# Queries and keys stacked along the contraction, through HBM, with no streamed matmuls ahead of the row scores

## What is computed

```
x = ln(x + splat_attention(x))        # 16-wide; scores = q_w . k_w, where q_w, k_w = exp(-distance to 16 centres)
x = ln(x + cross_attention(x, ctx))   # 16-wide, 120 keys
x = ln(x + one_of_8_experts(x))
x = ln(x + causal_attention(x))       # 16-wide, with biases
x = ln(x + block(x, ctx))             # self attention (32-wide, masked after the softmax) and an MLP,
                                      # then cross attention (32-wide, 120 keys) and an MLP
x = ln(x + four_of_16_experts(x))
attention: softmax(scale * q k^T) v, for each head
```

## Time and profile before

| | |
|---|---|
| median of three runs | 3835.8 us (3827.08 to 3843.56) |
| profiled execution | span 3842.1 us from the first to the last instruction; no separate time of the execution is given beside it |
| TensorE matmul busy | 3304.1 us, 86% of the span, 38960 instructions |
| VectorE, ScalarE, GpSimd busy | 2753.4, 2095.4 and 976.8 us |
| mean granted TensorE clock | 0.909 of 2.4 GHz |
| moved by DMA | 31.49 MB |

### The profile page before, as it was taken

One profiled execution on the slowest core, in us unless ns is written; L12 is line 12 of the kernel. 1 busy time (PEld: TensorE's weight loads), 2 busy tenths in 40 slices (PEclk: granted clock), 3 DMA queues, 4 the chain that ended last, 5 costly groups with the idle time before them and its releaser, 6 DMA issues. The chain is left out here.

```text
span 3842.1 us, 94561 instructions
## 1 busy us (share of the span) xinstructions
PE 3304.1 (86%) x38960; PEld 2345.7 (61%) x38960; DVE 2753.4 (72%) x6299; ACT 2095.4 (55%) x4222; POOL 976.8 (25%) x1792
## 2 busy tenths in 40 slices
PE   2989888889888888888988888899988898988886
PEld 1666666666665656666656666576655665666664
DVE  6777776777766767777767677677776777777755
ACT  5645655555456564564465555545555555466552
POOL 1312341122223321231133122212342122124310
PEclk9899998999989999999989898899988998999987
DMA  5000000000000000000000000000000000000000
GB/s 168 3 3 2 2 3 5 10 8 3 2 2 4 5 3 7 7 3 2 7 2 2 5 4 8 6 4 2 2 2 3 10 10 4 2 2 2 2 4 6
DMA packets 30365, 31.49 MB, mean 8 GB/s; under 512 B 8673, under 2 KB 26482, under 8 KB 29938
## 3 DMA queue, kind: packets, MB, share of 16 engines
q1 hardware_dynamic: 29938, 25.44, 2.2%
HBM read 21.24 MB, written 4.19 MB: 7 GB/s over the span
## 5 line engine op out<-in xcount | busy, mean ns | idle before, releaser
L1142 ACT ACTIVATE p<-bank,p_log 128x512 f32<-128x512 f32 (+2 forms) x1280 | 747.6, 584 | 1238.8 <-PE bank L834 1188.6
L1716 POOL TENSOR_TENSOR prob<-p,prob 120x256 f16<-120x256 f32 (+2 forms) x512 | 453.3, 885 | 1734.7 <-ACT prob L1143 1733.5
L1143 ACT ACTIVATE prob<-bank,p_log 128x512 f16<-128x512 f32 (+2 forms) x1280 | 748.2, 585 | 0.0
L1418 DVE TENSOR_REDUCE negm<-bank 128x2 f16<-128x512 f32 (+1 forms) x1280 | 675.5, 569 | 26.7 <-PE bank L789 15.6
L1336 DVE TENSOR_TENSOR prob<-p,prob 128x512 f16<-128x512 f32 (+2 forms) x768 | 467.4, 616 | 179.4 <-ACT prob L1143 175.7
L811 PE MATMUL bank<-q,k 32*128 32x256 f16 (+2 forms) x6144 | 491.0, 286 | 70.8 <-ACT prob L1143 28.0
L701 PE MATMUL bank<-w_exp,ident_h 128*128 128x512 f16 x1280 | 425.2, 417 | 16.6 <-DVE xa L1330 12.2
L1725 POOL TENSOR_SCALAR_AFFINE_SELECT probm<-prob 128x128 f16<-128x128 f16 x1024 | 328.1, 359 | 314.9 <-DVE prob L1336 314.9
L811 PEld LDWEIGHTS bank<-q,k 32*128 32x128 f16 (+1 forms) x6144 | 305.1, 109 | 150.2 <-issue 42.0
L834 PE MATMUL bank<-ident_h,negm 128*128 128x256 f16 (+2 forms) x2560 | 379.8, 270 | 0.0
L1708 POOL TENSOR_TENSOR rstd<-veps,minus_half 128x2 f32<-128x2 f32 (+2 forms) x192 | 146.3, 762 | 809.8 <-DVE veps L1304 809.1
(11 more groups left out here) (300 smaller groups left out, 6223.5 us busy)
## 6 DMA issues: line engine op xcount, KB each, us to landing
x<-in_x SPq DMA_DIRECT2D x16, 256.0 KB, 2.6
out<-z SPq DMA_DIRECT2D x16, 256.0 KB, 2.1
x<-in_li SPq DMA_DIRECT2D x7, 256.0 KB, 4.5
xa<-in_li SPq DMA_DIRECT2D x7, 256.0 KB, 4.5
z<-in_li SPq DMA_DIRECT2D x6, 256.0 KB, 4.6
x<-in_wq SPq DMA_DIRECT2D x4, 256.0 KB, 4.4
cx<-in_ctx_t SPq DMA_DIRECT2D x16, 60.0 KB, 1.8
cx<-in_ctx SPq DMA_DIRECT2D x16, 60.0 KB, 1.8
```

What stands on the lines that cost most here:

```text
L1142: act(p32[0:n, g % PBUF32, 0:cols], ps[0:n, 0:cols], ACT.Exp, bias=p_log[0:n, :], scale=a.scale)
L1143: act(prob[0:n, 0, g % PBUF, 0:cols], ps[0:n, 0:cols], ACT.Exp, bias=p_log[0:n, :], scale=a.scale).then_inc(a_done, one(a_done))
L1418: v.tensor_reduce(negm[:, h * NT:(h + 1) * NT], ring_v[bank_of(e, v_full)][:, :].rearrange("p (t n) -> p t n", t=NT)[:, :, 0:ATTNS[k].keys ...
L1716: g.tensor_tensor(prob[0:n, 1, m % PBUF, 0:cols], p32[0:n, m % PBUF32, 0:cols], prob[0:n, 0, m % PBUF, 0:cols], ALU.subtract).then_inc(pp_ ...
```

## The change

- Query and key parts of a head are stacked along the contraction. A stack of a 32-wide head has three planes, 96 rows: queries high, low, high against keys high, high, low. One of a 16-wide head has four planes and 16 rows of zeros, 80 rows: queries high, low, high, low against keys high, high, low, low. One matmul over the stack gives what three gave (with low by low added in the 16-wide ones).
- Row scores use the same stacks, so they are no longer of the high parts only. The heads of a pair come one after the other, as whole-height matmuls; `heads_of`, `at` and `parity` go.
- [...] `made` (one buffer, no longer two sets) takes the pair of parts; SP's queue stores each plane of it into `heads16` or `heads32` (four or three transfers for q, the same for k). `fill` brings four heads (a quad) back into one of three slots of `q_ring` and `k_ring`, two transfers a quad, four quads a phase. 
- ScalarE (in the splat attention VectorE) waits before it writes q into `made` until the keys of the phase before are stored, and before k until q is stored. A fill waits until k is stored, and for a slot until the exact scores of the quad three earlier are issued. PE waits for `ring_full` at each fourth head.
- Keys are made once. Those of the first cross attention take the short way from the bank; the causal ones are copied high by ScalarE.
- Exact scores are computed before the wait for the maxima, not after it.
- `STREAM_ROWS` is 0 instead of 2.
- At the start GpSimd clears a tile and SP writes eight transfers of zeros from it into the stacks' last 16 rows.

```diff
-STREAM_NORM, STREAM_GATES, STREAM_HEADS, STREAM_ROWS = 0, 0, 0, 2
+QUAD, QUADS, SLOTS = 4, 4, 3
+Q_PLANES = (0, 1, 0, 1)
+K_PLANES = {3: (0, 0, 1), 4: (0, 0, 1, 1)}
+STREAM_NORM, STREAM_GATES, STREAM_HEADS, STREAM_ROWS = 0, 0, 0, 0
...
-        qT = [pair(f"q{s}", 4, TOK) for s in range(SETS)]
-        kT = [pair(f"k{s}", 4, TOK) for s in range(SETS)]
+        made = pair("made", 4, TOK)
+        q_ring, k_ring = (sb(f"{what}_ring", [96, SLOTS, QUAD, TOK], F16) for what in "qk")
+        heads16 = {what: nc.dram_tensor(f"{what}_heads16", (2, 8, 80, 2, TOK), F16).ap() for what in "qk"}
+        heads32 = {what: nc.dram_tensor(f"{what}_heads32", (2, 4, 96, 4, TOK), F16).ap() for what in "qk"}
...
+                    for g in pair:
+                        a = ATTNS[ORDER[g][0]]
+                        if g % QUAD == 0:
+                            e.wait_ge(ring_full[g // QUAD % SLOTS], slot_filled(g // QUAD))
+                        q, kk = operands(g)
+                        ps = slot("v", "max", g)
...
+                        for i in range(NT):
+                            n = P if a.causal and i == 0 else a.keys
+                            last = mm(ps[:, i * TOK:i * TOK + n], q[:, i * P:i * P + P], kk[:, 0:n],
+                                      start=i == 0, stop=i == NT - 1 and not a.causal)
...
+                        for j, (k0, n) in enumerate(a.key_tiles):
+                            i0 = j * P if a.causal else 0
+                            mm(ps[0:n, j * TOK:j * TOK + TOK - i0], kk[:, k0:k0 + n], q[:, i0:TOK],
+                               start=j == 0, stop=False)
+                        e.wait_ge(*moved("max", g))
...
+                        for what, n, bias in (("q", TOK, bq2[:, 0:2]), ("k", a.keys, bq2[:, 2:4])):
+                            if stored_ahead(k, b, what) > 0:
+                                e.wait_ge(stored, stored_ahead(k, b, what))
+                            if a.causal:
+                                raw_tiles(a.tiles, n, made, bias)
+                            else:
+                                for m in range(0, a.tiles, 2):
+                                    highs((made[:, 0, m:m + 2, 0:n], lambda ps: two(ps)[:, :, 0:n], 1 / W_SCALE))
+                            yield
...
+                def store(what, k, b):
+                    a, p = ATTNS[k], PHASE[k, b]
+                    e.wait_ge(*was_split(what, k, b))
...
+                    to = heads_dram(what, k, b)
+                    for plane, part in enumerate(Q_PLANES[0:a.planes] if what == "q" else K_PLANES[a.planes]):
+                        e.dma_start(to[:, plane * a.dim:(plane + 1) * a.dim].rearrange("c d t n -> c d (t n)"),
+                                    made[:, part, 0:a.tiles, :].rearrange("p t n -> p (t n)")).then_inc(stored, 16)
+
+                def fill(quad):
+                    k, b = PHASES[quad // QUADS]
+                    a, n = ATTNS[k], quad % QUADS
+                    if n == 0:
+                        e.wait_ge(stored, STORED[k, b, "k"])
+                    if quad >= SLOTS:
+                        e.wait_ge(*moved("ring", quad - SLOTS))
+                    for what, ring, cols in (("q", q_ring, TOK), ("k", k_ring, a.keys)):
+                        t, c = (n, 0) if a.dim == 32 else (n // 2, n % 2 * QUAD)
+                        e.dma_start(ring[0:a.stacked, quad % SLOTS, :, 0:cols],
+                                    heads_dram(what, k, b)[c:c + QUAD, :, t, 0:cols].rearrange("c r n -> r c n")
+                                    ).then_inc(ring_full[quad % SLOTS], 16)
```

More of the change, by code:

```diff
@@ L390, in decoder @@
         out_done = [semaphore(f"out{s}_done") for s in range(2)]
+        zeros_made, zeros_stored = semaphore("zeros_made"), semaphore("zeros_stored")
+        stored = semaphore("stored")
+        ring_full = [semaphore(f"ring_full{slot}") for slot in range(SLOTS)]
         counts = Counts()
@@ L780, in row_scores @@
[L780 to L792, removed]
@@ L1366, in split_xT @@
                     lows(xT[:, 1], xT[:, 0])
[L1368 to L1386, removed]
+                def split_heads(a, what, k, b):
+                    n = a.keys if what == "k" else TOK
+                    if not a.splat and not a.causal:
                         for m in range(0, a.tiles, 2):
-                            lows(kk[:, 1, m:m + 2, 0:n], kk[:, 0, m:m + 2, 0:n],
+                            lows(made[:, 1, m:m + 2, 0:n], made[:, 0, m:m + 2, 0:n],
@@ L1389, in split_keys @@
                                  lambda ps: ps[:, :].rearrange("p (t n) -> p t n", t=2)[:, :, 0:n], 1 / W_SCALE)
                         return
[L1391 to L1394, removed]
-                            for t in range(KT):
[L1396 to L1400, removed]
+                    at = next_half(what, k, b)
@@ new lines, in split_heads @@
+                    tiles = raw[:, at:at + a.tiles, 0:n]
+                    if a.causal:
+                        last = low_part(made[:, 1, 0:a.tiles, 0:n], tiles, made[:, 0, 0:a.tiles, 0:n])
+                    else:
+                        if stored_ahead(k, b, what) > 0:
+                            e.wait_ge(stored, stored_ahead(k, b, what))
+                        if what == "q":
+                            last = split(tiles, made[:, 0, 0:a.tiles, :], made[:, 1, 0:a.tiles, :])
+                        else:
+                            for t in range(KT):
+                                last = split(raw[:, at + t, 0:n], made[:, 0, t, 0:n], made[:, 1, t, 0:n],
+                                             k_scale[:, t:t + 1])
@@ new lines, in _ @@
+                sends = [(at, chain, stage) for (chain, stage), at in PLACE.items()]
+                for p, (k, b) in enumerate(PHASES):
+                    for what in ("q", "k"):
+                        sends.append((PLACE[(k, b), what] + 0.5, (k, b), "store " + what))
+                    for quad in range(p * QUADS, (p + 1) * QUADS):
+                        begin = max((2 * quad - 4) * TURNS + 2, PLACE[(k, b), "k"] + 0.5)
+                        sends.append((begin + 0.1, quad, "fill"))
@@ L1811, in _ @@
+                for _, chain, stage in sorted(sends, key=lambda item: item[0]):
+                    if stage == "fill":
+                        fill(chain)
+                        continue
                     k, b = chain
+                    if stage[0:5] == "store":
+                        store(stage[6:], k, b)
                     following = NEXT[b]
```

106 lines of the change are left out of this document (50 added, 56 removed).

## The result

The changed kernel takes 4140.5 us (median of four runs, 4134.4 to 4143.7), 304 us more than before: ratio 1.078, 95% interval 1.075 to 1.081. The forecast was 3761 with a range up to 3900. It was wrong in sign and in range.

The account below looks back on a forecast made before the run. No single engine was taken to set all of it, TensorE being busiest at 86%. 3842.1 - 295 (TensorE work) + 175 (store waits) + 45 (clock) = 3767 us of span, 3761 as a median; range 3560 to 3900.

Parts of the forecast that it names:

- the size of the waits: Detour of queries and keys through HBM: waits for stores and ring fills add 175 us, 29 with fast stores.
- The causal ones and the longer self ones have three turns and more: nothing: Causal and longer self attentions: turns between making q and k hide the store, so no wait was counted.
- ahead of a copy that nothing needs for a phase; I take 1 us: First cross attentions: ScalarE waits up to 4.7 us before copying k; 1 us counted each, 16 in all.
- I take four fifths: Of 218 us of store waits, 175 counted, since TensorE's existing waits lie beside some of it.
- the clock: TensorE's granted clock: 22 long waits each add a slow stretch losing 2 us, 45 us; matmul changes cancel.
- the 96 us (640 x 0.15): TensorE's score matmuls: stacked operands save 0.15 us a pair over 640 pairs, including array switches.
- 57% reaches the end: Windows of 14 us: of 518 us taken from TensorE, 295 us or 57% shortens the kernel.
- The base (518): TensorE's time removed: 0.66 us streamed matmuls plus 0.15 us scores a pair, 518 us in all.
- the time of a store: Stores of q or k to HBM: 10 us for 32-wide heads, 4.7 us for 16-wide ones.
- Waits at full price: Rival, 17%: 11.7 us a store and nothing absorbed, 266 us of waits instead of 175, 3852 us.
- The clock falls without the streamed matmuls: Rival, 18%: TensorE's clock drops and the kernel ends slower; gain gone below 0.87, 3891 us at 0.84.
- Fast stores: Rival, 22%: all 16 engines carry the stores to HBM, so waits are small; 3575 us as a median.

Follow-up runs that it names:

- e9: The changed kernel without the stores of queries and keys, weights standing in HBM from the start, fills and other work kept: 3683.0 us, ratio 0.959.
- e2: The kernel before with no streamed matmuls, nothing else changed: 3951.6 us, ratio 1.029.
- the lean one: The changed kernel with each operand stored once, in one transfer of 128 rows, and copies of planes made by the fills: 3816.3 us, ratio 0.993.
- e5: The lean one with two streamed matmuls a pair put back: 3787.0 us, ratio 0.986.
- e4: The run of the lean one: one store of 128 rows per operand, fills plane by plane, against the changed kernel; 3816.3 us, ratio 0.993.
- e10: The lean one with 96 rows instead of 80 under the 16-wide scores, the added rows being zeros: 3784.9 us, ratio 0.985.
- e7: The lean one with 64 rows instead of 80 in the 16-wide stacks, without their rows of zeros: 3955.6 us, ratio 1.031.
- e8: The lean one without stores of queries and keys, the fills bringing weights stored at the start: 3676.5 us, ratio 0.958.

## Why the prediction was wrong

The sum was 3842 - 295 + 175 + 45. e9 splits what was measured into two parts: all but the storing, 3841 - 3683 = 158 us gained (forecast 295 - 45 = 250, with the whole clock term counted here), and the storing, 457 us lost (forecast 175). Their errors, 92 and 282, make the 379 us between 3761 and 4140.5 but for 5.

**Failed: the size of the waits**, 175 us, by two sentences.
- "The causal ones and the longer self ones have three turns and more: nothing", and of the first cross ones "ahead of a copy that nothing needs for a phase; I take 1 us". A turn is 47 / 32 = 1.5 us. The causal copies have three turns, 4.4 us, for a store of 6.1; the longer self ones have five, 7.3 us, for one of 11.3; the longer first cross ones have one, for 6.1. That leaves 1.7, 4.0 and 4.6 us a phase, where 2.3, 6.8 and 5.0 were measured. And nothing needs the copy, but ScalarE's queue is in order: the exponentials behind it are needed at once, and so VectorE and TensorE stand still. These groups cost 68 + 50 + 36 + 68 = 222 us (table at e9, whose sum is 461 for 457) against 13. The prediction named this very queue for the self attentions, and didn't apply it to the others. In the six short first cross attentions the ring is late as well (six of the twenty waits for it).
- "I take four fifths", since existing waits lie beside. In sum nothing was absorbed: the short self attentions were 23.6 us longer each, which is TensorE's 9.0 + 10.4 us of idle time and, behind each of the two in the timeline of one of them, some 4 to 5 us of matmuls at 1.2 GHz, of which half is lost (19.4 + 2 x 2.2 = 23.8, an estimate); 18.4 x 0.8 = 14.7 was counted. For them and the second cross ones together 232 us against 154.

**Failed: the clock**, 45 us with "the wider matmuls and the missing streamed ones I let cancel". They don't. Taking the streamed ones out costs 112 us in the kernel before (e2) and 29 in the lean one (e5 to e4). That the stacks of 80 and 96 rows stand in for the rest is argued from e10 and not shown: at 64 rows the streamed ones give only 17. In e9 the time at 1.2 GHz is (1 - 0.878) / 0.5 x 3682.8 = 899 us, 200 more than before, hence 100 us of TensorE's time if it is busy throughout them: 3304 - 425 + 100 = 2979, and it was busy 2983.8, where about 2800 was forecast. By that sum nothing is left of the 96 us (640 x 0.15) that I took for the scores. The rows, read again, say why: from the streamed matmuls to the maxima a splat pair took 1.50 us before (93.41 to 94.91) and takes 0.88 now. That is 0.62 us less, where 0.53 + 0.15 was counted at full clock (the change to 32 rows was in the 0.53 already) and 0.81 with the 0.66, which also holds the time in which the streamed ones overlap the next (0.59 us long, 0.53 to the next start). For all pairs 640 x 0.62 / 0.909 = 437 us is an estimate from the splat pair alone, near the 420 that go by the sum for e9 (3304 + 100 - 2984). The prediction read 0.97 against 1.74 us as a sign of parallel blocks and of the price of a change alike; it shows only the first, and the price, 0.10 us, shows in e5 and e7.

**Near right: 57% reaches the end.** From before to e9 TensorE is busy 320 us less and the kernel is 158 shorter, 49%. The base (518) was further off than the share.

**Near right: the time of a store**, 10 and 4.7 us; 11.3 and 6.1 measured, and the 1.4 us missing at 16-wide heads count in each of their waits. 768 KB in 11.3 - 1.2 us are 76 KB/us, four times the 18.8 of one engine that the earlier trace rows gave. The rule of the Trainium skill ("DMA: Bandwidth & Descriptors", Why a DMA increments its semaphore by 16 and not by 1), 4 engines for 4 blocks, gives 3 x 3.5 + 1.2 = 11.7 us as an estimate, and the trace agrees with 11.3. For 8 blocks the same estimate is 4.7, and 6.1 was measured. The three stores cost 3 x 0.57 us of issue, where I took 0.45 each, and the four of a 16-wide operand 2.43. Of bytes, q1 moved 227.68 MB where I had some 100; no term of the sum used that.

**The rivals.** "Waits at full price" had the mechanism and gave 3852: its price was right (11.7), its list of attentions as short as the forecast's. "The clock falls without the streamed matmuls" happens, but 0.878 (e9) is above the 0.87 under which it would decide; 0.825 in the changed kernel comes with the waits, since e4, with the same matmuls, runs at 0.856. "Fast stores", 3575, is refuted by the 11.3 us, and by e8 and e9 too: with no stores at all the time is 3677 and 3683.

## What to carry to other kernels

A store to HBM that a compute engine waits for holds up every instruction queued behind the wait on that engine. Count each such wait, also where nothing needs its result soon: take the time of the store, in microseconds, less the time between its issue and the write that waits for it. Lay the transfer out with 128 rows outermost on both sides and let the reading side make copies: here that edit, with fewer bytes stored, was worth 324 us. And before filler matmuls or rows of zeros go, price them by the clock: in the kernel before, the filler alone was worth 112 us.

## What the runs showed of the chip

- A change between a matmul block of 64 rows and one of 128 costs 0.10 us at full clock, and so does one from 128 to 32; one between 80 or 96 and 128 costs nothing that the starts show (before, after, e4, e5, e7).
- Three stores of 256 KB take 11.3 us when their outermost dimension in HBM has 4 blocks, and some 3.4 us with 128 rows (after, e9).
- Rows of zeros in the array count for the clock: 80 to 96 rows under 48 of 80 attentions took it from 0.856 to 0.875 and the time down by 31 us (e4, e10).
- TensorE's busy time can grow when work is taken out: 3304.1 to 3317.5 us without 425 us of matmuls (e2).
